# Numerator transfers of an attention kernel issued by ScalarE behind its copy, denominator transfers by SP

## What is computed

```python
x = _layernorm(x + _L0_attn_ref(x, ...))              # causal self attention, 112 keys
x = _layernorm(x + _L0_xattn_ref(x, ctx_1024, ctx_1024, mask, ...))   # 375 keys
x = _layernorm(x + _L0_ffn_ref(x, w_gate, w_up, w_down))
# in both attentions, per head:
attn = jax.nn.softmax(scores, axis=-1)
out = jnp.einsum('bhqk,bkhd->bqhd', attn, V)
```

## Time and profile before

| | us |
|---|---|
| median of 3 runs | 618.01 |
| lowest and highest | 613.01, 618.46 |
| the profiled execution | 618.47 |
| its span in the trace | 616.7 |

### The profile page before, as it was taken

How to read it: one execution, slowest core, us unless ns; L and a number is a source line. 1 busy time by engine, 2 the same in 40 slices (tenths; PEclk the granted TensorE clock), 3 DMA queues, 4 the chain that set the end, 5 groups by cost and what they waited for, 6 DMA issues and landing times.

```text
span 616.7 us, 16430 instructions
## 1 busy us (share of the span) xinstructions
PE 550.6 (89%) x5724; PEld 352.7 (57%) x5724; DVE 511.2 (83%) x1444; ACT 285.9 (46%) x671; POOL 177.2 (29%) x251
## 2 busy tenths in 40 slices
PE   3887798889999999999999998898999998898875
PEld 2544364546566666666665656564666655454543
DVE  3687877787898989898999997576989997788994
ACT  1342245356454554555545545544455455534412
POOL 7013141423131413323241414151232415121211
PEclk9998899699999999999999998997999999999999
DMA  8456544434553453627263634545262626230000
GB/s 253 118 155 196 151 147 129 131 115 132 147 154 91 121 165 108 177 85 200 74 175 86 186 95 134 157 117 161 84 190 76 171 86 182 63 115 16 27 7 26
DMA packets 75933, 77.14 MB, mean 125 GB/s; under 512 B 13068, under 2 KB 67404, under 8 KB 75852
## 3 DMA queue, kind: packets, MB, share of 16 engines
q1 hardware_dynamic: 73612, 73.75, 42.1%
q10 hardware_dynamic: 2240, 2.35, 1.3%
HBM read 39.89 MB, written 27.00 MB: 108 GB/s over the span
## 4 chain that ended last, share of the span: by engine, by line
PE 51%; DVE 27%; issue 9%; ACT 4%; DMA 4%; POOL 3%; SPq 2%; DVEq 0%; POOLq 0%; ACTq 0%
PE misc L2250 16%; PE misc L2236 8%; DVE junk L1432 4%; PE prob L2175 4%; PE score L2166 3%; PE xpv L2225 3%; PE prob L2181 3%; PE misc L2291 3%; PE apv L2213 3%; DVE xden L1471 2%; DVE amax L1424 2%; PE score L2142 2%; DVE qt L1348 2%; DVE qt L1338 2%; DVE xq L1350 1%
## 5 line engine op out<-in xcount | busy, mean ns | idle before, releaser
L1432 DVE CUSTOM_DVE_ANT_0 junk<-score,maskbias 112x375 bf16<-112x375 f32 x256 | 128.9, 542 | 25.8 <-PE score L2166 25.3
L932 ACT ACTIVATE xP<-prob 128x448 f32<-128x448 f32 (+1 forms) x192 | 94.0, 541 | 52.6 <-PE prob L2181 52.3
L2250 PE MATMUL misc<-wguT,xqT 128*128 128x352 f32 x224 | 80.2, 486 | 1.9 <-ACT xqT L892 1.1
L741 POOL TENSOR_TENSOR move_a<-mT,eye 128x448 bf16<-128x448 bf16 x32 | 36.2, 1150 | 73.5 <-ACT mT L892 73.5
L2166 PE MATMUL score<-xK,xQ 64*128 64x375 f16 x256 | 51.3, 333 | 6.7 <-DVE xmax L1432 2.8
L761 POOL TENSOR_TENSOR aattT<-anum,aden 128x224 f32<-128x224 f32 x16 | 10.9, 682 | 156.3 <-DVE aden L1471 86.2
L765 POOL TENSOR_TENSOR rstd<-veps,half 128x1 f32<-128x1 f32 (+1 forms) x44 | 28.0, 637 | 94.7 <-DVE veps L1507 94.6
L741 POOL TENSOR_TENSOR move_x<-mT,eye 128x448 bf16<-128x448 bf16 x32 | 33.2, 1043 | 74.4 <-ACT mT L892 74.4
L2250 PEld LDWEIGHTS misc<-wguT,xqT 128*128 128x128 f32 x224 | 39.0, 191 | 25.5 <-issue 8.2
L2250 PE MATMUL misc<-xwvT_s,ctxT_s 128*128 128x256 f32 (+1 forms) x192 | 50.6, 397 | 1.4 <-ACT kcf L892 1.1
L2225 PE MATMUL xpv<-xP,xV 128*32 128x112 f32 (+1 forms) x1536 | 51.3, 267 | 0.5 <-ACT xP L932 0.3
(11 more groups left out here) (159 smaller groups left out, 1099.0 us busy)
## 6 DMA issues: line engine op xcount, KB each, us to landing
xk_dram<-xk_parts SPq DMA_DIRECT2D x64, 192.0 KB, 3.2
xK<-xk_dram SPq DMA_DIRECT2D x16, 768.0 KB, 4.6
ctxT_s<-in_ctxT SPq DMA_DIRECT2D x15, 375.0 KB, 3.6
aq_dram<-aq_parts SPq DMA_DIRECT2D x64, 64.0 KB, 2.4
ak_dram<-ak_parts SPq DMA_DIRECT2D x64, 64.0 KB, 2.5
aQ<-aq_dram SPq DMA_DIRECT2D x16, 256.0 KB, 2.9
aK<-ak_dram SPq DMA_DIRECT2D x16, 256.0 KB, 2.9
xq_dram<-xq_parts SPq DMA_DIRECT2D x64, 64.0 KB, 2.1
```

The costliest lines, as they stand in the source:

```text
L741: pool.tensor_tensor(dst[:, big], mT[:, n, big].rearrange("p (j q) -> p j q", j=2).unsqueeze(2).to_broadcast([P, 2, GH, HS]), eye[:].unsqu ...
L932: act.activation(xP[0:KEYS[c], g % 2, c], prob[m][0:KEYS[c], 0:GH * S].rearrange("p (h q) -> p h q", h=GH), ACT.Exp).then_inc(probs.taken[ ...
L1432: dve.tensor_tensor_reduce(junk[:, m], score[m][0:S, 0:SC], maskbias[:], 1.0, -3.0e38, ALU.add, ALU.max, xmax[:, b.par, h // (2 * GH), h / ...
L2250: mm = pe.matmul(misc[m][0:rows_, 0:cols], actT(c), weightT(c), start=(c == 0), stop=(c == DT - 1))
```

## The change

`spread` on SP issues only the two transfers of the denominators. The two of the numerators are issued by ACT at the end of `pv_out`: ACT waits for the end of its own copy, waits for POOL's previous product, and issues. The transfers, their sources and the semaphores that they raise are the same.

```diff
@@ -537,9 +537,8 @@
                 sp.nop(nofuse=True)
                 wait_if(sp, att_ready[n], b.times(1, 0))
                 sp.nop(nofuse=True)
-                for odd, dst, landed in ((1, den[n], den_in[n]), (0, num[n], num_in[n])):
-                    for e in range(2):
-                        sp.dma_start(dst[HALF * e:HALF * e + HALF], src[odd:P:2, DT * e:DT * e + DT]).then_inc(landed, 16)
+                for e in range(2):
+                    sp.dma_start(den[n][HALF * e:HALF * e + HALF], src[1:P:2, DT * e:DT * e + DT]).then_inc(den_in[n], 16)
 
             def put_xq(i, b):
                 miscs.wait_taken(sp, i, "A.q")
@@ -1000,6 +999,12 @@
                     wait_if(act, landed, b.times(32, 0))
                     act.nop(nofuse=True)
                 copy(dst[:], pv[:, 0:GROUPS * S].rearrange("p (g q) -> p g q", g=GROUPS)).then_inc(ready, 1)
+                act.wait_ge(ready, b.times(1, 1))
+                act.nop(nofuse=True)
+                wait_if(act, att_ready[n], b.times(1, 0))
+                act.nop(nofuse=True)
+                for e in range(2):
+                    act.dma_start(num[n][HALF * e:HALF * e + HALF], dst[0:P:2, DT * e:DT * e + DT]).then_inc(num_in[n], 16)
 
             def take(i, label, dst, n=DT, w=S):
                 m = miscs.wait_full(act, i, label)
```

## The result

The changed kernel takes 639.1 us in the median of three runs (635.4 to 642.9), before 618.2 us in that of four (613.0 to 621.2). Its fourth run, 647.8 us, was in a slower state with a lower granted clock (0.951) and does not enter the comparison; with it the median is 641.0. The ratio is 1.035, with a 95% interval of 1.030 to 1.040: 3.5% slower, some 21 us. The runs of either kernel differ among themselves by over 1%. The profiled execution is the fastest, 635.37 us with a span of 633.5, 16.9 us above the profiled one of before. What follows is read from it.

A forecast was written before the change was run, and what follows sets the result against it. The chain ran mostly through PE, then DVE, with hardly any slack in either. Ten slots at 1.1 us (11) plus 7.2 outside them made 18.2 on 618, forecast 636 us; its own range 627 to 646, widened to 626 to 650.

The forecast's parts named there:

- the price of a slot: In each of the ten repeating slots, PE's delay lengthens the slot by 1.1 us; +11 us in all.
- the loose ends: Before 180 and behind 513.5 us, the twelve remaining copies cost 7.2 us together, with bounds of 2 and 11.
- The hold: Behind the self attention's copy, ACT waits 0.14 us and issues for 1.20 before the two exponentials can start.
- The cover: Before PE's group at 330.80, PE could have started at 330.48: 0.32 us of slack.
- The crossing to DVE: At 336.16 DVE takes PE's scores at the first moment it can, so the 1.1 us arrives in full.
- Rival 2: At the crossing to DVE part is absorbed, leaving 0.5 us a slot: about 625 us; chance 0.08.
- The other copy: Behind the cross attention's copy in a slot, ACT's idle time covers the delay: 0; without it another 1 us.
- The removal from SP: Two numerator issues behind each of 32 copies leave SP; gain 0, as denominators and their reciprocal stay as before.
- rival 1: SP's and ACT's sequencers take turns, so ACT is held 2.4 us a copy: 653 us; chance 0.13.
- 1.0, 1.7 and 2.0: In the ramp, at 94.80, near 134 and near 155 us: the microseconds lost at each.
- 1.4 and 1.1: In the end: 1.4 us for PE's wait for hqT behind the last copy, 1.1 for the end's other copies.
- Rivals 3 and 4: ACT is not held: 617.5 us, chance 0.04; the numerators' late landing was what mattered: 614 or less, chance 0.03.

The follow-up runs named there:

- cross_only: Against the kernel before, ACT issues the numerators of the cross attention only, SP the rest; 626.0 us, ratio 1.012.
- dummy_hold: Against the kernel before, SP keeps all transfers; ACT waits for its copy and copies it twice into an unread scratch tile; 643.0 us, ratio 1.044.
- late_issue: Against the kernel before, ACT issues the self attention's numerators in the ten slots only, behind the two exponentials; 618.9 us, ratio 1.006.
- slots_only: Against the changed kernel, ACT issues numerators in the ten slots alone, SP in the ramp and the drain; 629.3 us, ratio 1.019.
- late_and_cross: Against the changed kernel, ramp and drain as before; in the ten slots the self attention's numerators are issued behind the two exponentials; 619.8 us, ratio 1.002.
- self_only: Against the kernel before, ACT issues the numerators of the self attention only, SP the rest; 637.3 us, ratio 1.031.
- four_on_act: Against the changed kernel, the denominators move to ACT too, so SP issues neither pair; 689.0 us, ratio 1.121.
- pool_self: Against the kernel before, POOL issues the self attention's numerators ahead of its product, SP the cross attention's; 623.4 us, ratio 1.009.
- wait_only: Against the kernel before, ACT gets only the two waits behind its copy; SP keeps all issues; 616.6 us, ratio 1.002.

## Why the prediction was right, point by point

The forecast was 636 us, within 626 to 650, slower; the measurement is 639.1. The mechanism and the price of a slot came out as worked out; one term, the loose ends, was too small.

- **The hold.** Worked out: 0.14 + 1.20 us, exponentials at 1.34 behind the copy's end. Measured: 0.14 + 1.13 and 0.05 more to the exponentials, at 1.32. The step from ACT's queue at the start of the program to the middle of it was sound.
- **The cover.** Worked out from the distance of 0.15 us between ACT's end and PE's start: 0.32 us. The experiments give 0.31.
- **The crossing to DVE.** Argued from the distance of 0.48 us in two places: nothing is absorbed. The slot grew by 1.09 us, the whole of PE's delay, and DVE shows idle time there. Rival 2 is out.
- **The other copy.** Entered at 0 for the slots: cross_only shows 33.50. The prediction gave no size for that cover, and it is narrow: the copy into kcf had 0.72 us of idle time before it, now begins 0.91 us later, and PE already waits 0.17 us for it.
- **The removal from SP**, entered at 0: no run shows a gain. PE's waiting for the product fell by 2.8 us, but in dummy_hold, where nothing was removed, by 2.5. The premise that the denominators are issued as before holds only nearly: SP's second issue got longer (rival 1, below), and those of the self attention land 2.2 us after their issue in the median where they took 1.9. In late_issue they take 2.2 too, at a slot of 33.51, so this costs the slot nothing.
- **The range.** Its upper end does not follow from its terms: 618.0 with ten times 1.15 and 11 for the loose ends gives 640.5, not 646. It was widened to 650 in any case, and 639.1 lies inside either.
- **The loose ends were mis-sized: 7.2 worked out, about 9 measured.** The ratios of the change and of slots_only are 1.035 and 1.019; the difference, 10 us with an uncertainty of some 5 us, is the ramp and the drain. The traces say where it lies, if stretches of equal granted clock are compared. First the ramp, from one self attention copy to the next: each time the kernel without a hold, then the change. The first line is from late_and_cross, whose ramp is that of before and had the clock of the change there. Behind the length stand busy times of PE, PEld, DVE, ACT and POOL, then the clock and the DMA.

```profile
93.63:128.19 34.56, 28.03 (x372) 17.85 (x364) 27.33 (x75) 16.58 (x38) 9.42 (x10) 0.95 0.53 150
92.83:129.45 36.62, 28.31 (x373) 17.70 (x367) 27.88 (x75) 16.57 (x38) 9.17 (x10) 0.95 0.50 143
```

```profile
131.47:153.86 22.39, 21.92 (x324) 14.01 (x316) 18.37 (x42) 14.81 (x35) 8.99 (x12) 1.00 0.41 115
129.45:153.95 24.50, 21.73 (x316) 13.88 (x315) 18.10 (x42) 14.89 (x35) 9.02 (x12) 1.00 0.38 106
```

```profile
153.86:194.54 40.68, 39.20 (x342) 25.46 (x342) 35.91 (x109) 20.01 (x49) 9.93 (x12) 1.00 0.51 142
153.95:196.95 43.00, 39.50 (x342) 25.40 (x342) 36.06 (x109) 20.01 (x49) 9.75 (x12) 1.00 0.49 135
```

The stretches are 2.1, 2.1 and 2.3 us longer, 6.5 in all, where the prediction had 1.0, 1.7 and 2.0. The step that failed most is the first: at 94.80 it let part of the hold be spent in a wait for the product, and the stretch grew by more than a whole hold. Its share of the cross attention's copy at 100.8, for which nothing was entered, is not separated. Then the drain, from the last self attention copy on, before and after:

```profile
528.06:616.70 88.64, 71.34 (x610) 42.77 (x609) 71.96 (x221) 32.05 (x72) 15.71 (x25) 1.00 0.15 44
538.95:633.50 94.55, 74.83 (x618) 44.62 (x610) 72.19 (x223) 32.15 (x72) 15.61 (x25) 0.96 0.14 41
```

Here the clocks differ, so I take the length less PE's busy time, 17.3 and 19.7 us. The 2.4 us between them are an estimate of what the hold costs there; the prediction had 1.4 and 1.1. Of the 1.4 the row came out: behind the last copy PE's wait for hqT grew from 1.05 us to 2.72, by 1.7.

```profile
593.67 3.05 PE L2341 MATMUL misc<-wdT,hqT 128*128 128x256 f32 x12 [2.72 <-ACT hqT L891]
```

- **What hid it in the profile.** The changed kernel's own trace shows only 2.4 us in the whole ramp, 194.5 to 196.9 us, and I would have read it as a smaller price. But the granted clock is not the same in two executions. Windows of the ramp, of before, of the change and of self_only:

```profile
0.00:194.50 194.50, 162.55 (x1592) 102.20 (x1594) 148.31 (x391) 81.64 (x192) 57.89 (x88) 0.94 0.53 151
```

```profile
0.00:196.90 196.90, 157.21 (x1592) 97.98 (x1594) 148.42 (x391) 81.63 (x192) 57.62 (x88) 0.97 0.53 149
```

```profile
0.00:201.40 201.40, 163.42 (x1592) 101.96 (x1594) 148.31 (x391) 81.75 (x192) 57.67 (x88) 0.94 0.52 146
```

With the same 1592 matmuls PE was busy 5.3 us less in the change than before, as more of it ran at 2.4 GHz. self_only, at the mean clock of before, took 201.4, 6.9 us more. Even equal means mislead: in self_only the reduced clock fell on the stretch between the fourth and the fifth copy, 26.35 us at 0.94, which is 24.50 in the change and 22.39 before at 1.00. So some 2 of the 6.9 us are clock. The opposite happened at the end: from the last slot's copy on, the change ran at 0.97 where before ran at 1.00. So 16.9 us in the pair of profiled executions and 21 us in the timed ones are both right; what repeats from trace to trace is the plain slot.

The lines of time against clock agree, as estimates at equal clock: slots_only lies 11 us above before (ten times 1.09 is 10.9), self_only 17, cross_only 5, dummy_hold 21. The clocks of the runs of before that belong to the change are not on record; against the lines of the other chips it lies about 20 above.

**Rival 1**, that the sequencers take turns for whole pairs, is out: ACT's pair takes 1.13 us beside SP's issues and 1.12 in four_on_act without them, not 2.4. Some disturbance exists. Where both queues issue, the one of the two second issues that starts later is longer by 0.25 us: behind the self attention's copy SP's (0.84 in place of 0.59), behind the cross attention's copy mostly ACT's (0.86 in place of 0.62). In late_issue SP's is as long, and the slot is 33.51, so it does not lengthen the slot. The lock described by the Trainium skill, "Perfetto Trace Analysis", section "DMA Instruction — HWDGE (DVE, Sync)", may be behind it; no run here isolates it. **Rivals 3 and 4** are out by the idle time before PE's line 2180 and by the 1.09 us.

The rule of the Trainium skill, "DMA: Bandwidth & Descriptors", section "Issuing engines are not separate DMA queues", is that only the issuer's time is saved. The trace agrees: the numerators are issued 1.2 us earlier, and from issue to landing those of the self attention take 2.0 us in the median, as before (those of the cross attention 2.2 against 2.0). What the rule leaves open is where that time is spent again.

What stays open: how the 2.1 us of the stretch near 95 us divide between the two copies in it, and why one landing of POOL's transfers in pool_self took so long, where the median of its 32 was 1.9 us.

## What to carry to other kernels

Before a transfer is given to a compute engine, look up what that engine does next and who waits for it: a delay of 1.4 us on an engine that is 46% busy cost 1.09 us in a slot, because the engine with the real work wanted its next result within 0.3 us. Put the issue behind the instructions that are urgent, not directly behind the one that makes the data: two instructions further back it started just as early and cost nothing in the slots. Compare a part that repeats by its own length in the traces: it showed differences of 0.1 us where the totals scatter by 1%. And a wait that vanished is not yet a gain: the numerators landed over a microsecond earlier, and the product that needed them started when it had before.

## What the runs showed of the hardware that I had not expected

ACT's queue issues a transfer while ACT still computes what was handed to it before: issues at 326.34 and 326.85 lie inside exponentials of 326.12 to 327.10. The issue held only the instructions behind it, not those ahead. Two waits without an issue delayed ACT's next instruction by 0.24 us (wait_only).

The kernel with the longest hold also had the lowest clock. four_on_act, with PE busy for 84% of its span, had a mean granted clock of 0.934. Five of its slots, with stretches at 1.2 GHz in them, were 38.3 to 38.6 us long, the two without 36.8. That is part of why its loss of 73 us is far more than the hold explains. That the clock fell because PE idled more is only argued: in its profiled execution the change idles more than before too, and its clock was not lower (0.978 against 0.972).
